# A two-layer attention kernel: the row shift moved to GpSimd, strided row maxima, and another order of the third slot

## The chip, the cores and the metric

One core of one Trainium2 chip runs the kernel; its seven other cores do nothing. The metric is the device time of one launch in microseconds. The times stand in a table below.

## What is computed

32 batches of 256 rows of 256 numbers go through two layers. Layer 0 is cross-attention (16 heads of 64, 77 keys per batch) and a gated feed-forward part, layer 1 is cross-attention with other weights and a matrix product with quantised operands. Ahead of each part the rows are normalised:

```python
def _layernorm(x, axis=-1, eps=1e-05):
    m = jnp.mean(x, axis=axis, keepdims=True)
    v = jnp.var(x, axis=axis, keepdims=True)
    return (x - m) / jnp.sqrt(v + eps)

x = x + _L0_xattn_ref(_layernorm(x, axis=-1), ctx_768, ...)   # softmax(q k^T / 8) v, then Wo and bo
x = x + _L0_ffn_ref(_layernorm(x, axis=-1), ...)              # (silu(x wg^T) * (x wu^T)) wd^T, hidden size 768
x = x + _L1_xattn_ref(_layernorm(x, axis=-1), ctx_768, ...)
x = x + _L1_ffn_ref(_layernorm(x, axis=-1), L1_ffn_rhs)       # rows scaled by max|x|/127, rounded, times rounded rhs
```

## The kernel before, in words

A first block loads and splits the weights and computes keys and values of all batches for both layers. The second block is the part that this case is about. Every number in single precision is held as a high half (float16) and a low half (the rest), so that most products are three matmuls: high by high, low by high, high by low.

The second block runs 66 **bodies**, h = 0 to 65. Bodies 0 to 31 attend in layer 0, bodies 32 to 63 in layer 1. A body has four **slots**, u = 0 to 3, and each slot takes four of the sixteen heads, a **unit**. Work is pipelined over slots and bodies. In slot u, TensorE computes

- the scores of unit u (`scores`, line 1211), into a buffer that has to be emptied by the exponentials of the unit before;
- the queries of the unit two slots on (`queries`, through `product`, line 328);
- the output projection of the unit four slots back (`project`);
- the product of probabilities and values of the unit three slots back (`weigh_values`, line 1245).

DVE takes the negated row maxima of the scores in two halves (`nmax`, line 1513), the reciprocals of the row sums (`rden`, 1518) and the low halves `oT_l` and `qT_l`. ACT computes the exponentials with their sums (`ex`, 1390), and high halves of everything (line 343). POOL (GpSimd) turns exponentials into probabilities: times the reciprocal into `pr` (1681), the cast into `p` (1694), the rest into the low half of `p` (1686). SP's queue turns the probabilities by a DMA transpose into `pT` (line 1099), once for each half of the rows.

Beside attention, a layer-0 body carries the feed-forward part of older batches: of batch h - 2 the gate products 0 to 3 and of batch h - 3 the gate products 4 and 5 and the two down products. One gate product is `gate_up(c)`, chunk c of 128 of the 768 hidden columns: matmuls of `wgT` and of `wuT` with `x2T`. After it come `tanh_gate` on ACT (`th`, 1370), `sigmoid_gate` and `hidden` on DVE (`sg`, 1480; `hf`, 1491), `high_hidden` on ACT (`hT_h`) and `low_hidden` on POOL or DVE (`hT_l`). `down(t)` multiplies by `wdT`, and `out_rows` adds it to `y` on DVE (1501).

The path of a batch through a body is this. At the end of slot 3 DVE adds projection and residual into `x1` (line 1661). It waits there for POOL's copy of the `x1` before into `y` (1723). Statistics follow (`spreads`, `moments`, lines 373 to 381), then on POOL the power -1/2 (`inverse`, line 396), on DVE the normalised rows `x2` (`normalise_rows`, 368), then `x216` in two halves (ACT 343, DVE 357), and a DMA transpose on SP into `x2T` (`turn_second_rows`, line 1107), which all gate products of that batch read. `x_pair` (lines 1177, 347) holds the first rows of a batch that is to enter, which ACT normalises with the scale `rs` and the shift `nmr`; `xT` (line 312) is their transpose.

`shift` makes `nmr`, minus mean times inverse deviation, on DVE (line 386), for the entering rows and for the rows `yn` that layer 0 hands on.

In layer 1, DVE computes `x2`, its row maxima `am` (1616), the scale `lsc` (1506) and its reciprocal `linv` (1509) in slot 1; ACT scales the rows into `q_a` (1424), DVE rounds them (`q_i`, 1553), TensorE turns and multiplies them.

The order of everything is written out by hand: each engine walks the slots, and inside a slot the `if u == ...` lines stand in the order in which its instructions run. No engine reorders. Banks of PSUM for queries, gate, down and turned products come from a plan made by `uses` and `released`; two banks serve the feed-forward products in turn.

## Time and profile before

| | us |
|---|---|
| median of 3 runs | 1621.58 |
| lowest and highest | 1621.55, 1623.29 |
| time of the profiled execution | 1628.16 |
| its span, first to last instruction | 1626.0 |
| TensorE matmul busy | 1522.9 (94%) |
| DVE busy | 1406.7 (87%) |
| ACT busy | 1315.0 (81%) |
| POOL busy | 1273.6 (78%) |
| mean granted TensorE clock | 0.993 |

A busy time is the time in which the engine has an instruction at work; an instruction may begin up to 0.1 us before the one ahead of it ends. The first 180 us or so are the first block. Bodies of layer 0 fill the time to about 1030, bodies of layer 1 the rest.

### The profile page before, as it was taken

The numbers are of one execution on the slowest core, as the hardware profiler recorded it, in microseconds if no ns is written. First come the engines' busy times: TensorE is split into PE (matmuls) and PEld (weight loads), VectorE is DVE, ScalarE is ACT, GpSimd is POOL, SyncE is SP. The second block draws the span as 40 slices with busy tenths as digits, with TensorE's granted clock in tenths as the row PEclk, the third lists the DMA queues.
The fourth block names the chain that finished last, engine by engine and source line by source line (L and its number), as shares of the span: only waits on it lengthen the run. The fifth ranks groups of instructions, "written<-read, shape, count | busy, mean of one in ns | idle before, by whom it ended". The sixth has DMA issues, their size and how long they took to land.

```text
span 1626.0 us, 74813 instructions
## 1 busy us (share of the span) xinstructions
PE 1522.9 (94%) x27282; PEld 1318.8 (81%) x27282; DVE 1406.7 (87%) x3585; ACT 1315.0 (81%) x5514; POOL 1273.6 (78%) x1893
## 2 busy tenths in 40 slices
PE   7999888999999999999999999999999999999995
PEld 4556578899998999899999889888788888788883
DVE  6777678899999999999999978889989989998986
ACT  6656588888888888888888878788888888888883
POOL 5100188899999999999999888788888888888884
PEclk9999999999999999999999999999999999999998
DMA  9997699887887787787788989898888888888995
GB/s 261 358 294 260 212 184 180 172 184 167 176 182 169 174 182 165 177 179 170 176 178 170 169 156 174 171 187 184 186 182 187 188 188 188 183 186 183 190 179 117
DMA packets 740021, 307.76 MB, mean 189 GB/s; under 512 B 629201, under 2 KB 725361, under 8 KB 737841
## 3 DMA queue, kind: packets, MB, share of 16 engines
q1 hardware_dynamic: 738049, 299.32, 83.0%
q0 software_dynamic: 1840, 6.82, 1.5%
q8 instruction: 67, 1.10, 0.3%
q14 instruction: 65, 0.53, 0.1%
HBM read 87.09 MB, written 65.54 MB: 94 GB/s over the span
## 4 chain that ended last, share of the span: by engine, by line
POOL 30%; DVE 19%; issue 14%; PE 12%; ACT 9%; DMA 3%; SPq 1%; DVEq 1%; POOLq 0%; ACTq 0%
POOL pr L1681 11%; ACT ex L1390 8%; PE psum L328 7%; POOL p L1694 6%; POOL p L1686 5%; POOL hT_l L1672 3%; PE psum L1211 3%; DVE qT_l L360 3%; DVE oT_l L357 3%; POOL rs L396 2%; DVE x L368 2%; DVE nmax L1513 2%; POOL x_res L1705 2%; DMA pT<-p 2%; DVE ya L1604 1%
## 5 line engine op out<-in xcount | busy, mean ns | idle before, releaser
L1390 ACT ACTIVATE ex<-psum,nmax 128x77 f32<-128x77 f32 x2048 | 634.7, 331 | 47.8 <-DVE nmax L1513 38.3
L1390 ACT ACTIVATION_READ_ACCUMULATOR ex<-psum,nmax 128x1 f32 x2048 | 433.6, 212 | 0.0
L1686 POOL TENSOR_TENSOR p<-pr,p 128x308 f16<-128x308 f32 x512 | 398.5, 779 | 38.3
L1681 POOL TENSOR_TENSOR pr<-ex,rden 128x308 f32<-128x308 f32 x512 | 390.4, 763 | 29.7 <-DVE rden L1518 29.5
L328 PE MATMUL psum<-xT,wq_h 128*64 128x256 f16 x4064 | 353.4, 276 | 0.0
L1694 POOL CAST p<-pr 128x308 f16<-128x308 f32 x509 | 247.4, 486 | 45.6 <-DMA pT<-p 13.6
L1513 DVE TENSOR_REDUCE nmax<-psum 128x4 f32<-128x308 f32 x512 | 236.8, 463 | 53.2 <-PE psum L1211 51.7
L328 PE MATMUL psum<-xT,wq_l 128*64 128x256 f16 x2032 | 281.0, 273 | 0.0
L328 PE MATMUL psum<-wo_h,oT_h 128*64 128x256 f16 x1792 | 249.9, 275 | 28.0 <-DVE oT_l L357 27.8
L328 PE MATMUL psum<-wo_l,oT_h 128*64 128x256 f16 x1792 | 248.4, 273 | 0.0
L328 PE MATMUL psum<-wo_h,oT_l 128*64 128x256 f16 x1792 | 248.4, 273 | 0.0
L328 PEld LDWEIGHTS psum<-xT,wq_h 128*64 128x64 f16 x4064 | 211.2, 110 | 12.2
L1245 PE MATMUL psum<-pT,vb 77*64 77x256 f16 x3072 | 212.4, 273 | 4.4 <-DMA pT<-p 4.3
L343 ACT ACTIVATE oT_h<-psum 128x512 f16<-128x512 f32 x256 | 153.6, 600 | 62.4 <-PE psum L1245 59.1
L1211 PEld LDWEIGHTS psum<-kb,qT_h 64*128 64x128 f16 x4096 | 114.7, 94 | 88.1 <-issue 88.1
L357 DVE TENSOR_TENSOR oT_l<-psum,oT_h 128x512 f16<-128x512 f32 x256 | 174.2, 681 | 2.6 <-ACT oT_h L343 2.6
L1245 PEld LDWEIGHTS psum<-pT,vb 77*64 77x64 f16 x3072 | 164.2, 109 | 14.6 <-issue 11.8
L1211 PE MATMUL psum<-kb,qT_h 64*128 64x77 f16 x4096 | 145.4, 197 | 31.4 <-ACT ex L1390 12.8
L360 DVE SCALAR_TENSOR_TENSOR qT_l<-psum,qT_h 128x512 f16<-128x512 f32 x256 | 173.9, 679 | 0.0
L343 ACT ACTIVATE qT_h<-psum 128x512 f16<-128x512 f32 x256 | 152.0, 594 | 3.0 <-PEq L406 3.0
L396 POOL TENSOR_TENSOR rs<-ve,half_neg 128x2 f32<-128x2 f32 x127 | 88.6, 697 | 81.0 <-DVE ve L381 78.0
L328 PEld LDWEIGHTS psum<-wo_h,oT_h 128*64 128x64 f16 x1792 | 102.1, 110 | 47.2 <-DVE oT_l L357 42.3
(164 smaller groups left out, 3477.6 us busy)
## 6 DMA issues: line engine op xcount, KB each, us to landing
keys<-ks SPq DMA_DIRECT2D x16, 1232.0 KB, 6.8
kb<-keys SPq DMA_DIRECT2D x256, 77.0 KB, 2.7
vb<-vals SPq DMA_DIRECT2D x128, 154.0 KB
vals<-vs SPq DMA_DIRECT2D x64, 256.0 KB, 4.1
x_pair<-in_x_dram SPq DMA_DIRECT2D x32, 256.0 KB, 3.0
pT<-p SPq DMA_TRANSPOSE x512, 3.2
x_res<-in_x_dram SPq DMA_DIRECT2D x32, 256.0 KB, 3.1
mid_x<-y SPq DMA_DIRECT2D x32, 256.0 KB, 2.4
```

The source lines that it names most:

```text
L328: last = pe.matmul(o[b * DH:(b + 1) * DH], w[:, b * DH:(b + 1) * DH], x, **flags)
L343: return act.activation(dst, src, ACT.Copy, scale=scale)
L357: return dve.tensor_tensor(dst, src, hi, ALU.subtract)
L360: return dve.scalar_tensor_tensor(out=qT_l[i][:, :, :], in0=src, scalar=Q_DOWN, in1=qT_h[i][:, :, :], op0=ALU.mult, op1=ALU.subtract)
L396: pool.tensor_tensor(rs[:, :], ve[:, :], half_neg[:, :], ALU.pow).then_inc(s_inv[k], 1)
L1211: last = pe.matmul(SC[:, b, at], w[rows, a, t * P:(t + 1) * P], kb[u // 2][rows, b, part, u % 2 * PPU + a, :], start=(q == 0), stop=(q == ...
L1245: last = pe.matmul(o[b * DH:(b + 1) * DH, a, :].rearrange("p (t q) -> p t q", q=P), vb[u // 2][:, part, c:c + DH], pT[u][0:NK, b, at:at + ...
L1390: last = act.activation(ex[i][:, t, b, :], SC[:, t, b * NK:(b + 1) * NK], ACT.Exp, bias=nmax[i][:, t, b:b + 1], accum_out=den[i][:, t, b:b ...
L1513: dve.tensor_reduce(nmax[i][:, t, :], SC[:, t, :].rearrange("p (h k) -> p h k", k=NK), AX_X, ALU.max, negate=True).then_inc(s_m, 1)
L1681: pool.tensor_tensor(pr[:, t, :, :], ex[i][:, t, :, :], r, ALU.mult).then_inc(s_p, 1)
L1686: pool.tensor_tensor(d[:, t, 1, :, 0:NK], pr[:, t, :, :], d[:, t, 0, :, 0:NK], ALU.subtract).then_inc(s_pl, 1)
L1694: pool.tensor_copy(p16[v % 2][:, t, 0, :, 0:NK], pr[:, t, :, :]).then_inc(s_ph, 1)
```

## The change

`shift` goes from DVE to POOL and takes two instructions there: minus the mean, and that times the inverse deviation, with a semaphore of its own (`s_neg`) between them. It stands directly behind `inverse` for the entering rows and for `yn`. POOL's `inverse` and `shift` of the entering rows come after the probabilities of slot 1 and not before them.

The row maxima `am` are written and read with a stride of two numbers.

In layer 0 the third slot (u = 2) is in another order. Gate product 0 leaves slot 1 and comes in slot 2, after queries and `down(0)`. The output projection stands before `down(1)` and gate product 1. On DVE the maxima, `oT_l` and the second maxima come first, then the statistics of the entering rows, the reciprocals, `qT_l`, and then `out_rows(0)` and the elementwise parts of gate product 0. On ACT both sets of exponentials come first. On DVE in slots 0 and 1, the low half of `x216` goes from the end of slot 0 to slot 1, and SP's `turn_second_rows` from slot 0 to the end of slot 1.

In layer 1, `normalise_rows` goes from slot 1 to slot 0, and `am`, `lsc`, `linv` stand before the low half of `xT`.

The core of the diff:

```diff
-        def shift(dve, k, mv, rs, count):
-
-            dve.wait_ge(s_inv[k], count)
-            dve.scalar_tensor_tensor(out=nmr[k][:, :], in0=mv[:, :, 0], scalar=-1.0, in1=rs[:, :],
-                                     op0=ALU.mult, op1=ALU.mult).then_inc(s_nmr[k], 1)
+        def shift(pool, k, mv, rs, count):
+
+            pool.tensor_scalar(nmr[k][:, :], mv[:, :, 0], -1.0, None, ALU.mult).then_inc(s_neg[k], 1)
+            pool.wait_ge(s_inv[k], count)
+            pool.wait_ge(s_neg[k], count)
+            pool.tensor_tensor(nmr[k][:, :], nmr[k][:, :], rs[:, :], ALU.mult).then_inc(s_nmr[k], 1)
...
-        am = sb("am", [P, QT], F32)
+        am = sb("am", [P, QT, 2], F32)
...
                         if turning:
                             turn_probabilities(n + u - 1, (u - 1) % UNITS, 0)
-                        if u == 0 and lay[-2] == 0:
-                            turn_second_rows(h - 2)
...
                         if turning:
                             turn_probabilities(n + u - 1, (u - 1) % UNITS, 1)
+                        if u == 1 and lay[-2] == 0:
+                            turn_second_rows(h - 2)
...
-                        if u == 1 and lay[-2] == 0:
-                            pe.wait_ge(s_x2d, 16 * (h - 1))
-                            if like == 2:
-                                pe.wait_ge(s_kvf, RING + LATE_BASE + LATE - 1)
-                            gate_up(0, bank("gu", 0))
...
+                        if u == 2 and lay[-2] == 0:
+                            pe.wait_ge(s_x2d, 16 * (h - 1))
+                            if like == 2:
+                                pe.wait_ge(s_kvf, RING + LATE_BASE + LATE - 1)
+                            gate_up(0, bank("gu", 0))
...
-                        if u == 0 and lay[-2] == 0:
-                            dve.wait_ge(s_x216h, h - 1)
-                            low(dve, x216[:, :, 1, :], x2[:, :, :], x216[:, :, 0, :]).then_inc(s_x216l, 1)
...
+                        if u == 1 and lay[-2] == 0:
+                            dve.wait_ge(s_x216h, h - 1)
+                            low(dve, x216[:, :, 1, :], x2[:, :, :], x216[:, :, 0, :]).then_inc(s_x216l, 1)
...
-                        if u == 1 and lay[-2] == 1 and like <= NB:
-                            normalise_rows(dve, 1, x2, x1, mv2, rs2, h - 1, s_x2)
...
+                        if u == 0 and lay[-2] == 1 and like <= NB:
+                            normalise_rows(dve, 1, x2, x1, mv2, rs2, h - 1, s_x2)
```

Three places, as the instructions stand in each engine's queue. The first is SP's queue in a layer-0 body, from the keys' load of slot 0 to the last probability transpose of slot 1 (`p_1` holds odd units, `p_0` even ones). Before:

```order
L302 DMA kb<-keys 64x616 x2
L1099 DMA_TRANSPOSE pT<-p_1 128x8x128
L1107 DMA_TRANSPOSE x2T<-x 128x8x128
L312 DMA_TRANSPOSE xT<-x 128x8x128
L1099 DMA_TRANSPOSE pT<-p_1 128x8x128
L1099 DMA_TRANSPOSE pT<-p_0 128x8x128
L1084 DMA vb<-vals 77x2x512
L1099 DMA_TRANSPOSE pT<-p_0 128x8x128
```

And now:

```order
L303 DMA kb<-keys 64x616 x2
L1100 DMA_TRANSPOSE pT<-p_1 128x8x128
L313 DMA_TRANSPOSE xT<-x 128x8x128
L1100 DMA_TRANSPOSE pT<-p_1 128x8x128
L1100 DMA_TRANSPOSE pT<-p_0 128x8x128
L1085 DMA vb<-vals 77x2x512
L1100 DMA_TRANSPOSE pT<-p_0 128x8x128
L1108 DMA_TRANSPOSE x2T<-x 128x8x128
```

The transpose into `x2T` has moved past `xT`, three probability transposes and the values' load.

The second is TensorE's queue in the layer-0 loop, around gate product 0. Before, it lies between the value product of slot 1 and the scores of slot 2:

```order
L328 MATMUL psum<-wo_l,oT_h 64x256 x2
L1245 MATMUL psum<-pT,vb 64x256 x12
L1347 REGISTER_ALU
L1293 REGISTER_ALU
L328 MATMUL psum<-x2T,wgT 64x256 x8
L328 MATMUL psum<-x2T,wuT 64x256 x8
L1198 REGISTER_ALU
L270 REGISTER_ALU
L1211 MATMUL psum<-kb,qT_h 128x77 x4
```

And now, between `down(0)` and the output projection of slot 2:

```order
L329 MATMUL psum<-wdT,hT_h 64x256 x2
L329 MATMUL psum<-wdT,hT_l 64x256 x2
L1320 REGISTER_ALU
L1294 REGISTER_ALU
L329 MATMUL psum<-x2T,wgT 64x256 x8
L329 MATMUL psum<-x2T,wuT 64x256 x8
L1220 REGISTER_ALU
L329 MATMUL psum<-wo_h,oT_h 64x256 x2
```

The gate product has moved behind the scores, the queries and the first down product.

The third is DVE's queue in the layer-1 loop, from `qT_l` of slot 0. Before:

```order
L360 SCALAR_TENSOR_TENSOR qT_l<-psum,qT_h 128x512
L1518 RECIPROCAL rden<-den 128x4 x2
L1512 ISA
L1513 TENSOR_REDUCE nmax<-psum 128x4
L1548 REGISTER_ALU
L357 TENSOR_TENSOR oT_l<-psum,oT_h 128x512
L1512 REGISTER_ALU
L1513 TENSOR_REDUCE nmax<-psum 128x4
L1599 REGISTER_ALU
L360 SCALAR_TENSOR_TENSOR qT_l<-psum,qT_h 128x512
L368 TENSOR_SCALAR x<-x,mv,rs 128x256 x2
```

And now:

```order
L361 SCALAR_TENSOR_TENSOR qT_l<-psum,qT_h 128x512
L369 TENSOR_SCALAR x<-x,mv,rs 128x256 x2
L1519 RECIPROCAL rden<-den 128x4 x2
L1513 ISA
L1514 TENSOR_REDUCE nmax<-psum 128x4
L1536 REGISTER_ALU
L358 TENSOR_TENSOR oT_l<-psum,oT_h 128x512
L1513 REGISTER_ALU
L1514 TENSOR_REDUCE nmax<-psum 128x4
L1586 REGISTER_ALU
L361 SCALAR_TENSOR_TENSOR qT_l<-psum,qT_h 128x512
L1607 TENSOR_REDUCE am<-x 128x2
```

The two rows of the normalisation (`x<-x,mv,rs`) have moved ahead of slot 1's maxima.

## Rows read from the trace of the kernel before

**Rows 1.** Busy time in a stretch of layer 0: PE, PEld, DVE, ACT, POOL, clock, DMA

```profile
400.00:500.00 100.00, 97.85 (x1956) 91.39 (x1952) 91.03 (x253) 87.19 (x368) 91.91 (x135) 1.00 0.80 175
```

**Rows 2.** Timeline of DVE, layer 0, two bodies' ends: start, duration, instruction

```profile
507.52 0.69 DVE L1661 SCALAR_TENSOR_TENSOR x<-psum,x_res 128x512 f32<-128x512 f32 x1 [0.24 <-POOL y L1723]
...
532.06 0.69 DVE L1661 SCALAR_TENSOR_TENSOR x<-psum,x_res 128x512 f32<-128x512 f32 x1 [0.23 <-POOL y L1723]
```

**Rows 3.** Timeline of POOL, the same body of layer 0, slots 0 and 1

```profile
509.88 0.69 POOL L396 TENSOR_TENSOR rs<-ve,half_neg 128x2 f32<-128x2 f32 x1 [0.48 <-DVE ve L381]
...
518.01 0.67 POOL L1672 TENSOR_TENSOR hT_l<-hf,hT_h 128x256 f16<-128x256 f32 x1 [0.34 <-ACT hT_h L343]
518.64 0.75 POOL L1686 TENSOR_TENSOR p<-pr,p 128x308 f16<-128x308 f32 x1
```

**Rows 4.** Timeline of TensorE, layer 1: projection and scores that waited

```profile
1309.50 0.30 PE L328 MATMUL psum<-wo_h,oT_h 128*64 128x256 f16 x2 [0.64 <-DVE oT_l L357]
...
1312.44 0.25 PE L1211 MATMUL psum<-kb,qT_h 64*128 64x77 f16 x4 [0.34 <-ACT ex L1390]
```

**Rows 5.** Timeline of DVE, layer 0, x216 and hidden chunk 5

```profile
513.33 1.10 DVE L357 TENSOR_TENSOR x<-x 128x512 f16<-128x512 f32 x1
...
517.06 0.42 DVE L1491 SCALAR_TENSOR_TENSOR hf<-psum,sg 128x256 f32<-128x256 f32 x1
```

**Rows 6.** Timeline of SP's queue, layer 0: issue of the transposes

```profile
514.45 1.23 SPq L1107 DMA_TRANSPOSE x2T<-x  x1
...
517.12 2.72 SPq L1099 DMA_TRANSPOSE pT<-p  x2
...
520.49 1.23 SPq L1099 DMA_TRANSPOSE pT<-p  x1
```

**Rows 7.** Tile x2T, from 340 to 880: DMA from issue to landing

```profile
DMA to landing us min/median/max: 3.2/3.2/3.6
```

**Rows 8.** Timeline of TensorE, layer 0, slot 2 (first row of each part)

```profile
518.75 0.24 PE L1211 MATMUL psum<-kb,qT_h 64*128 64x77 f16 x4
...
520.62 0.39 PE L328 MATMUL psum<-xT,wq_h 128*64 128x256 f16 x4
...
521.93 0.28 PE L328 MATMUL psum<-wdT,hT_h 128*64 128x256 f16 x2
...
523.24 0.60 PE L328 MATMUL psum<-x2T,wgT 128*64 128x256 f16 x8
...
524.11 0.28 PE L328 MATMUL psum<-wo_h,oT_h 128*64 128x256 f16 x2
...
525.42 0.82 PE L1245 MATMUL psum<-pT,vb 77*64 77x256 f16 x12
526.18 0.24 PE L1211 MATMUL psum<-kb,qT_h 64*128 64x77 f16 x4
```

**Rows 9.** Timeline of ACT, layer 0: tanh and high parts of hidden chunks

```profile
501.23 0.42 ACT L343 ACTIVATE hT_h<-hf 128x256 f16<-128x256 f32 x1 [0.22 <-DVE hf L1491]
...
505.63 0.36 ACT L1370 ACTIVATE th<-psum 128x256 f32<-128x256 f32 x1
...
524.32 0.38 ACT L1370 ACTIVATE th<-psum 128x256 f32<-128x256 f32 x1 [0.51 <-PE psum L328]
...
525.75 0.42 ACT L343 ACTIVATE hT_h<-hf 128x256 f16<-128x256 f32 x1 [0.22 <-DVE hf L1491]
```

**Rows 10.** Busy time in four microseconds near 940, columns of rows 1

```profile
940.00:944.00 4.00, 4.00 (x60) 3.48 (x58) 1.89 (x6) 2.64 (x11) 2.90 (x4) 0.57 0.97 196
```

**Rows 11.** Timeline of TensorE, the wait ahead of that

```profile
938.88 0.63 PE L328 MATMUL psum<-x2T,wgT 128*64 128x256 f16 x8 [1.86 <-DMA x2T<-x]
```

**Rows 12.** Line L577, a small addition on POOL: duration min/median/max in ns

```profile
L577 POOL TENSOR_TENSOR ve<-mv,eps x1: 191/191/191, 165.5 to 165.5; 128x2 f32<-128x2 f32 x1
```

**Rows 13.** Line L368, the normalised rows, whole trace: duration min/median/max in ns

```profile
L368 DVE TENSOR_SCALAR x<-x,mv,rs x126: 401/634/996, 237.3 to 1603.0; 128x256 f32<-128x256 f32 x126
```

**Rows 14.** Timeline of DVE, layer 1: first maxima of slot 1

```profile
1302.81 0.48 DVE L1513 TENSOR_REDUCE nmax<-psum 128x4 f32<-128x308 f32 x1 [0.72 <-PE psum L1211]
```

More of the change, by code:

```diff
@@ L280, in xattn_ffn_kernel @@
         s_inv = [sem(f"s_inv{i}") for i in range(3)]
+        s_neg = [sem(f"s_neg{i}") for i in range(3)]
         s_nmr = [sem(f"s_nmr{i}") for i in range(3)]
@@ L580, in _ @@
                 inverse(pool, 0, ve1, rs1, 1)
+                shift(pool, 0, mv1, rs1, 1)
             @block.scalar
@@ L1010, in uses @@
                         out.append(("turned_x", 0))
-                    if lay[-2] == 0:
-                        out.append(("gu", 0))
                 if u == 2:
@@ L1015, in uses @@
                         out.append(("down", 0))
+                    if lay[-2] == 0:
+                        out.append(("gu", 0))
                     if lay[-3] == 0:
@@ L1301, in body @@
                             scores(n + u, u, 32 * (h + 1))
-                        if u == 2 and lay[-3] == 0:
-                            pe.wait_ge(s_hlp, len(LOW_POOL) * (h - 2))
-                            pe.wait_ge(s_hld, len(LOW_DVE) * (h - 2))
-                            down(0, bank("down", 0))
                         if u == 3 and lay[-2] == 0:
@@ L1317, in body @@
                                 quantised(t, bank("quant", t))
+                        if u == 2 and lay[-3] == 0:
+                            pe.wait_ge(s_hlp, len(LOW_POOL) * (h - 2))
+                            pe.wait_ge(s_hld, len(LOW_DVE) * (h - 2))
+                            down(0, bank("down", 0))
+                        if u == 2 and lay[-2] == 0:
[3 more added lines that the diff above has]
+                            gate_up(0, bank("gu", 0))
                         if u == 0 and lay[-3] == 0:
@@ L1337, in body @@
                             project(n + u - 4, u, four)
+                        if u == 2 and lay[-3] == 0:
+                            down(1, bank("down", 1))
+                        if u == 2 and lay[-2] == 0:
+                            if like == 2:
+                                pe.wait_ge(s_kvf, RING + LATE_BASE + LATE)
+                            gate_up(1, bank("gu", 1))
                         if u == 2 and lay[-2] == 1:
@@ L1455, in body @@
                             exponentials(n + u, u % 2, 1)
+                        if u == 2 and lay[-2] == 0:
+                            tanh_gate(0, h - 2)
+                        if u == 2 and lay[2] == 0:
+                            act.wait_ge(s_nmr[0], h + 2)
+                            act.wait_ge(s_x16l, h + 1)
+                            normalise(act, xn, x_in, rs1, 0, s_xn)
                         if u == 1 and lay[-3] == 0:
@@ L1600, in body @@
                             low_q(dve, (u + 1) % 2, RG[(u + 1) % 2]).then_inc(s_ql, 1)
+                        if u == 2 and lay[-3] == 0:
+                            out_rows(0)
+                        if u == 2 and lay[-2] == 0:
+                            sigmoid_gate(0, h - 2)
+                        if u == 2 and lay[-2] == 0:
+                            hidden(0, h - 2)
+                        if u == 1 and lay[-2] == 0:
+                            dve.wait_ge(s_x216h, h - 1)
+                            low(dve, x216[:, :, 1, :], x2[:, :, :], x216[:, :, 0, :]).then_inc(s_x216l, 1)
+                        if u == 1 and lay[-3] == 0:
+                            sigmoid_gate(5, h - 3)
+                        if u == 1 and lay[-3] == 0:
+                            hidden(5, h - 3)
+                        if u == 1 and lay[-3] == 0:
+                            low_hidden(4, h - 3)
+                        if u == 0 and lay[-2] == 1 and like <= NB:
+                            normalise_rows(dve, 1, x2, x1, mv2, rs2, h - 1, s_x2)
+                        if u == 1 and lay[-2] == 1 and like <= NB:
+                            dve.wait_ge(s_x2, QT * (h - 1))
+                            dve.tensor_reduce(am[:, :, 0], x2[:, :, :], AX_X, ALU.max,
+                                              apply_absolute_value=True).then_inc(s_am, 1)
+                            quantising_scale(h - 2 - B)
                         if u == 3 and lay[-2] == 1:
@@ L1723, in body @@
                             pool.tensor_copy(y[:, :, :], x1[:, :, :]).then_inc(s_yx, 1)
-                        if u == 1 and lay[2] == 0:
-                            inverse(pool, 0, ve1, rs1, h + 2)
                         if (like, u) == (NB - 1, 3):
@@ L1730, in body @@
                             probabilities(h, u, 0)
+                        if u == 1 and lay[2] == 0:
+                            inverse(pool, 0, ve1, rs1, h + 2)
+                            shift(pool, 0, mv1, rs1, h + 2)
                         if u == 2 and lay[-3] == 0:
                             inverse(pool, 2, ve3, rs3, h - 2)
+                            shift(pool, 2, mv3, rs3, h - 2)
                         if u == 2 and lay[-2] == 0:
```

55 lines of the change are left out of this document (11 added, 44 removed).

## The prediction

> **What bounds the kernel now.** I read the stretches first, then one body of each layer on each engine, then who waited for whom. In layer 0 the matmuls cover 97.9% of a stretch at full granted clock [rows 1], so little can be gained there: the additions into `x1` of two neighbouring bodies stand at 507.52 and 532.06, a body of 24.6 us with the clock at 1.00, and in both DVE waits 0.2 us for POOL's copy into `y` [rows 2]. TensorE, DVE and POOL are all nearly full, so what matters is no engine's sum but the loop that a body closes over several engines: `x1`, its row statistics, the inverse deviation on POOL (509.88, it waited for DVE's `ve` [rows 3]), POOL's probabilities in program order, the pieces of the feed-forward part, the next `x1`. Layer 1 has slack on every engine and loses time in small waits, such as 0.64 us before the output projection and 0.34 us before the scores [rows 4].
>
> **The turn of the second rows (layer 0).** This is the main term. `x2T`, the turned second rows, is what every gate product reads. Before, SP issues that transpose in the first slot, at 514.45, as soon as DVE has `x216`. Now it stands behind the second probability transpose of the second slot. That one waits for POOL's last piece of unit 0, and SP takes its queue strictly in order. When is that piece ready? POOL's inverse starts at 509.88, 2.36 us after `x1`. From there POOL works in order until the subtraction of 518.64, 0.75 us long, ends at 519.39: 9.51 us [rows 3]. POOL's `hT_l` ahead of it (518.01) needs the hidden chunk 5 of DVE, 517.06. DVE's 1.10 us subtraction `x216` moves from 513.33 to a place in front of that chunk. DVE then idles first, for the scores of unit 1; I estimate +0.3 us [rows 5]. Then the `pT` transpose occupies SP 1.25 us (520.49), `x2T` follows it, and lands 3.2 us after its start [rows 6, 7]. From `x1` to the first possible gate product: 2.36 + 9.51 + 0.3 + 1.3 + 3.2 + 0.1 for the hand-overs = **16.8 us**, that is 524.3 on the clock of these rows.
>
> When would TensorE like to have it? The first gate product (0.87 us, as 523.24 to 524.11) no longer stands ahead of the scores at 518.75. They move up by it and by some 0.45 us of waits in unit 1 (DVE's `x216` had stood in front of that unit's maxima), to about 517.4. Scores and one down product take 1.87 us, queries 1.31, so the gate product's turn comes at 520.6 [rows 8]. It waits 3.7 us in an in-order queue, with output projection, second down and gate product, and value product all behind it.
>
> The loop from there: gate 0.87, projection 1.31, down 1.31 until the second gate product starts (3.5); 1.08 to its tanh (523.24 to 524.32), 1.43 to the high part of the second hidden chunk (525.75), 4.40 from such a copy to the last tanh of the fourth slot (501.23 to 505.63), 1.65 to `x1` (507.52 without the 0.24 us for POOL) [rows 2, 8, 9]. 16.8 + 3.5 + 1.08 + 1.43 + 4.40 + 1.65 = 28.9 us, the upper end. The lower end counts the lateness once: second slot ends at 524.3 + 0.87 + 1.31 + 1.31 + 0.87 + 0.76 = 529.4 instead of 526.18, +3.3, less the 0.24 us: 27.7. The difference is that the second gate product now stands right before the value product, so its elementwise chain starts later against the fourth slot. I take 28.3, since small waits inside the upper chain can close: **+3.7 us a body**. 31 bodies hold this product, and one or two next to the change of layers already have slack: 30 x 3.7 = **+111 us** (ends 93 and 129).
>
> **TensorE's clock.** A stop of 3.7 us (part of it taken earlier, before the queries) in every body is new. Around 938.88 the trace has one wait of 1.86 us for this very transpose, and the granted clock of the next four microseconds is 0.57, so nearly all at 1.2 GHz [rows 10, 11]. At 0.57 in 4 us, 4 x (1 - 0.57) = 1.7 us of work are lost, and what follows the wait is the critical chain. I take it for six bodies in ten: 30 x 0.6 x 1.7 = **+30 us** (ends 0 and 51). The Trainium skill, TensorE: Matmul & The Clock Gate, section HAM oscillation, tells of a kernel whose every tile waits for a DMA, and whose every next tile starts at half clock; by that rule all 30 bodies would pay, +51 in place of +30, and the forecast would be 1771. The same page, Part 1, puts the ramp under 1% of a typical kernel, at most some 16 us here; by that 1736. No row here has a regularly repeated stop.
>
> **Mean times inverse deviation on POOL.** Two per layer-0 body: DVE loses two small instructions, POOL gains four, with a wait of its own between them. The nearest rows are POOL's 128x2 addition at 0.19 us and the 128x2 power at 0.69 [rows 3, 12]: 0.8 to 2.8 us a body. In the old loop this would be serial, since DVE waits for POOL's `y` at `x1`. In the longer loop POOL gets idle time ahead of the third inverse, which now waits for later statistics. I book 0, and up to 0.5 us a body at the dearer end (+15 on the high side).
>
> **Layer 1.** The normalisation of the second rows moves from behind the maxima of unit 1 to the end of unit 0, and scale and reciprocal come ahead of `xT`. The pair of rows costs 2 x 0.63 us at the median, 2 x 0.40 or 2 x 1.00 at the ends [rows 13]. It lands in the 0.72 us that DVE idles before the maxima at 1302.81 [rows 14], and starts after POOL's inverse, about 1302.2. So these maxima start at 1303.6, 0.8 us late; unit 1's exponentials and the next scores follow by as much. Against that the scale is ready over a microsecond earlier, so ACT no longer waits for it in unit 2. The projection at 1309.50 waited for DVE [rows 4] and starts as before; the exponentials of unit 2 end before TensorE asks, so the 0.34 us before 1312.44 and about 0.1 beside them go: -0.42 us a body, 30 bodies, **-13 us**. At 0.40 a row everything moves up by half a microsecond more, about -1.0 a body (-29); at 1.00 it turns to +0.14 (+4). The strided maxima save part of a small instruction that is off this path: 0.
>
> **Sum.** +111 + 30 - 13 = +128 against the profiled execution's own 1628.2, which is 6.6 us over the median; against the median, 1621.6 + 128 = **1750 us**.
>
> **The rivals.**
> - The turn is late, but the clock holds: 1621.6 + 111 - 13 = 1720. For it: other stretches with waits stay at full clock. Chance 0.28.
> - POOL is what counts: `x2T` comes in time after all, because POOL runs ahead, and only the four small instructions lengthen POOL's loop, by 0.8 us at least: 1621.6 + 24 - 13 = 1633, and 1690 at the dearer price. Against it: POOL waits for `ve` at 509.88 in each body, so it can't run ahead of `x1`. Chance 0.09.
> - Faster. The mechanism is the third slot itself: with maxima first and gate product behind, 0.45 us of waits a body go. It decides if SP issues `x2T` by 517.3, 3.3 us ahead of 520.6; SP would then need POOL's piece by 516.0, 3.4 us before 519.39 [rows 3]. The price: 1621.6 - 30 x 0.45 - 13 = 1595. Chance 0.07.
> - It does nothing measurable: turn and shorter waits cancel. 1621, chance 0.03.
>
> **How the numbers follow.** The forecast (late turn and half clock in many bodies) has 0.53, and with its bounds spans about 1725 to 1790. 1690 to 1785 takes in the clock that holds and the lower end of the loop (1621.6 + 93 - 29 = 1686), and leaves the cases below and the dearest sum out. A difference of 0.2%, some 3 us, is what a measurement of this kernel can tell from none. Faster by more than that 0.07, within it 0.03, slower 0.90.
>
> **What would show it.** In the profile after: layer-0 `x1` additions 28 us apart or more; TensorE idle before a gate product with the DMA into `x2T` as releaser, about 3 us in each body; SP's `x2T` directly behind a `pT`, some 13.5 us after `x1`; granted clock under 1.00 in layer 0's stretches; layer-1 bodies near 18.5 us; ACT's wait for the scale gone. If the bodies of layer 0 stay under 25 us, the loop as I drew it is wrong; if TensorE waits for `x2T` but the clock reads 1.00, only the clock term falls.

## The result, and the profile after

The changed kernel takes **1786.73 us** (median of 5 runs, 1783.84 to 1795.86) against 1621.55 us of the kernel before in the same job. The ratio is 1.102, with a 95% interval of 1.1001 to 1.104: 165 us slower. 1750 was forecast, with a range of 1690 to 1785. The sign, the place and the main mechanism are as forecast; the size lies 1.7 us above the range, and the profiled execution, 1795.86 us, 11 us above it.

The stretches come first, one of each layer (columns as in [rows 1]: length, PE, PEld, DVE, ACT, POOL busy, granted clock, DMA share, GB/s).

```profile
400.00:500.00 100.00, 82.39 (x1518) 75.97 (x1516) 67.57 (x190) 66.46 (x285) 77.01 (x124) 0.94 0.66 144
1400.00:1500.00 100.00, 95.76 (x1843) 83.55 (x1840) 92.89 (x232) 85.00 (x410) 87.83 (x137) 1.00 0.87 192
```

Layer 0 lost 15 us of TensorE's 98 in a hundred and has a granted clock of 0.94 where [rows 1] had 1.00. Everything is less busy, POOL too (77 where it was 92): no engine became the bound, a wait did. Layer 1 gained. The chain that ended last (first by engine, then its largest lines) says the same, with a DMA among the lines:

```profile
POOL 28%; issue 18%; PE 16%; DVE 9%; SPq 9%; DMA 7%; ACT 2%; POOLq 0%; DVEq 0%; ACTq 0%
PE psum L329 14%; POOL pr L1680 11%; POOL p L1693 7%; SPq L1100 6%; DMA x2T<-x 6%; POOL p L1685 4%; POOL rs L391 2%; SPq L313 2%; POOL hT_l L1671 2%; DVE x L369 1%; PE psum L1212 1%; DMA pT<-p 1%; DVE sg L1481 1%; POOL y L1722 1%; DVE x L1660 1%
```

The waits of the whole span (who waited for whom, us in total, times, longest):

```profile
ACT th L1371 <- PE psum L329: 261.9, 65, 6.3
POOL rs L391 <- DVE ve L382: 232.1, 96, 15.4
...
PE psum L329 <- DMA x2T<-x: 106.5, 32, 4.1
```

32 waits of TensorE for `x2T`, 3.3 us each: one in every body of layer 0. ACT's and POOL's sums were 56.2 and 78.0 us before; the body below shows both waiting in the wake of the same stop.

One body of layer 0 in the timelines, of DVE (its two `x1` additions; answers to [rows 2]), POOL ([rows 3]), SP ([rows 6]), TensorE ([rows 8]) and ACT ([rows 9]), with start, duration and, in brackets, idle time before and what ended it:

```profile
568.89 0.69 DVE L1660 SCALAR_TENSOR_TENSOR x<-psum,x_res 128x512 f32<-128x512 f32 x1 [0.24 <-POOL y L1722]
...
599.29 0.69 DVE L1660 SCALAR_TENSOR_TENSOR x<-psum,x_res 128x512 f32<-128x512 f32 x1 [0.24 <-POOL y L1722]
```

```profile
571.25 0.72 POOL L391 TENSOR_TENSOR rs<-ve,half_neg 128x2 f32<-128x2 f32 x1 [0.48 <-DVE ve L382]
...
579.89 0.67 POOL L1671 TENSOR_TENSOR hT_l<-hf,hT_h 128x256 f16<-128x256 f32 x1 [1.11 <-ACT hT_h L344]
580.51 0.76 POOL L1685 TENSOR_TENSOR p<-pr,p 128x308 f16<-128x308 f32 x1
...
583.90 0.22 POOL L395 TENSOR_SCALAR nmr<-mv 128x2 f32<-128x2 f32 x1
584.27 0.20 POOL L398 TENSOR_TENSOR nmr<-nmr,rs 128x2 f32<-128x2 f32 x1
584.42 1.26 POOL L1704 TENSOR_TENSOR x_res<-x_res,bo_b 128x512 f32<-128x512 f32 x1
...
594.13 1.12 POOL L391 TENSOR_TENSOR rs<-ve,half_neg 128x2 f32<-128x2 f32 x1 [4.46 <-DVE ve L382]
```

```profile
581.37 1.24 SPq L1100 DMA_TRANSPOSE pT<-p  x1
582.71 1.29 SPq L1108 DMA_TRANSPOSE x2T<-x  x1
```

```profile
580.00 0.41 PE L329 MATMUL psum<-xT,wq_h 128*64 128x256 f16 x4 [0.82 <-DMA xT<-x]
...
586.04 0.63 PE L329 MATMUL psum<-x2T,wgT 128*64 128x256 f16 x8 [3.24 <-DMA x2T<-x]
586.50 0.98 PE L329 MATMUL psum<-x2T,wuT 128*64 128x256 f16 x8
```

```profile
587.60 0.38 ACT L1371 ACTIVATE th<-psum 128x256 f32<-128x256 f32 x1 [4.37 <-PE psum L329]
...
592.30 0.38 ACT L1371 ACTIVATE th<-psum 128x256 f32<-128x256 f32 x1 [3.35 <-PE psum L329]
```

The body is 30.40 us long, where it was 24.54. POOL's last piece of unit 0 ends at 581.27, SP turns it at 581.37, and only then `x2T`, at 582.71, 13.8 us after `x1` (forecast 13.5). The first gate product stands at 586.04, 17.15 us after `x1` (forecast 16.8), after a stop of 3.24 us. And it runs slow: eight products of `wuT` take 0.98 us where eight of this shape took 0.60 in [rows 8]. The clock of four-microsecond stretches of this body shows it:

```profile
580.00:584.00 4.00, 2.81 (x48) 2.54 (x48) 3.34 (x11) 3.23 (x18) 3.86 (x7) 1.00 0.99 198
584.00:588.00 4.00, 1.96 (x24) 1.83 (x26) 0.00 (x0) 0.40 (x2) 3.70 (x7) 0.82 0.87 174
588.00:592.00 4.00, 4.00 (x60) 3.80 (x58) 1.38 (x4) 0.96 (x2) 1.52 (x3) 0.75 0.35 66
592.00:596.00 4.00, 4.00 (x90) 3.74 (x86) 3.76 (x12) 3.43 (x12) 1.72 (x4) 1.00 0.68 171
```

4 x (1 - 0.82) + 4 x (1 - 0.75) = 1.7 us of work are lost, the same 1.7 as taken from [rows 10]. In stretches of one microsecond the clock reads 0.96 from 586 to 587, 0.50 in each of the next three, and 1.00 from 590 on: it falls to 1.2 GHz behind the stop, when TensorE is already at work again.

In how many bodies does the clock fall? Of the 33 distances between neighbouring `x1` additions in layer 0, 28 are between 29.3 and 31.2 us and five are under 29. The granted clock from one `x1` to the next tells it directly: it is 0.89 to 0.95 in 30 of the 33 bodies, and 1.00 in three of 28.6 to 28.9 us. This is the profiled execution, 9 us above the median, with a mean granted clock of 0.960 where the other four have 0.965 to 0.969, so in the median execution some bodies fewer will have fallen.

The length of the stop doesn't tell a body that falls from one that does not. The first of these two gate products of the changed kernel belongs to a body with the clock at 1.00, the second to one with 0.94:

```profile
526.87 0.63 PE L329 MATMUL psum<-x2T,wgT 128*64 128x256 f16 x8 [3.14 <-DMA x2T<-x]
...
920.22 0.63 PE L329 MATMUL psum<-x2T,wgT 128*64 128x256 f16 x8 [3.15 <-DMA x2T<-x]
```

Layer 1 has bodies of 18.37 us against 18.87 to 18.95 before.

### The profile page after: what moved, and what is told of

Its sections match the earlier page's. It is cut to its first block, busy times and chain, and to the rows that moved or that the text cites. A ratio compares the mean times of both kernels' runs of the same rounds, so it can differ in the third digit from the quotient of the medians.

```text
span 1793.9 us, 74939 instructions
## 1 busy us (share of the span) xinstructions
PE 1576.5 (88%) x27282; PEld 1360.7 (76%) x27282; DVE 1379.9 (77%) x3522; ACT 1295.0 (72%) x5514; POOL 1287.2 (72%) x2019
## 3 DMA queue, kind: packets, MB, share of 16 engines
q8 instruction: 68, 1.11, 0.3%
## 4 chain that ended last, share of the span: by engine, by line
POOL 28%; issue 18%; PE 16%; DVE 9%; SPq 9%; DMA 7%; ACT 2%; POOLq 0%; DVEq 0%; ACTq 0%
PE psum L329 14%; POOL pr L1680 11%; POOL p L1693 7%; SPq L1100 6%; DMA x2T<-x 6%; POOL p L1685 4%; POOL rs L391 2%; SPq L313 2%; POOL hT_l L1671 2%; DVE x L369 1%; PE psum L1212 1%; DMA pT<-p 1%; DVE sg L1481 1%; POOL y L1722 1%; DVE x L1660 1%
## 5 line engine op out<-in xcount | busy, mean ns | idle before, releaser
L1391 ACT ACTIVATION_READ_ACCUMULATOR ex<-psum,nmax 128x1 f32 x2048 | 454.4, 222 | 0.0
L1680 POOL TENSOR_TENSOR pr<-ex,rden 128x308 f32<-128x308 f32 x512 | 382.4, 747 | 22.7 <-DVE rden L1519 22.6
L329 PE MATMUL psum<-wo_h,oT_h 128*64 128x256 f16 x1792 | 265.8, 291 | 8.1 <-DVE oT_l L358 6.1
L1693 POOL CAST p<-pr 128x308 f16<-128x308 f32 x509 | 237.0, 466 | 45.3 <-DMA pT<-p 13.2
L391 POOL TENSOR_TENSOR rs<-ve,half_neg 128x2 f32<-128x2 f32 x127 | 100.2, 789 | 232.5 <-DVE ve L382 232.1
L1371 ACT ACTIVATE th<-psum 128x256 f32<-128x256 f32 x192 | 75.8, 395 | 262.0 <-PE psum L329 261.9
L329 PE MATMUL psum<-wo_h,oT_l 128*64 128x256 f16 x1792 | 263.8, 289 | 0.0
L329 PE MATMUL psum<-wo_l,oT_h 128*64 128x256 f16 x1792 | 262.9, 288 | 0.0
L329 PE MATMUL psum<-x2T,wgT 128*64 128x256 f16 x1536 | 123.8, 285 | 106.5 <-DMA x2T<-x 106.5
L1481 DVE SCALAR_TENSOR_TENSOR sg<-th,psum 128x256 f32<-128x256 f32 x192 | 79.4, 413 | 156.6 <-ACT th L1371 154.1
```

Of the source, the lines that this page charges most:

```text
L329: last = pe.matmul(o[b * DH:(b + 1) * DH], w[:, b * DH:(b + 1) * DH], x, **flags)
L391: pool.tensor_tensor(rs[:, :], ve[:, :], half_neg[:, :], ALU.pow).then_inc(s_inv[k], 1)
L1391: last = act.activation(ex[i][:, t, b, :], SC[:, t, b * NK:(b + 1) * NK], ACT.Exp, bias=nmax[i][:, t, b:b + 1], accum_out=den[i][:, t, b:b ...
L1680: pool.tensor_tensor(pr[:, t, :, :], ex[i][:, t, :, :], r, ALU.mult).then_inc(s_p, 1)
L1693: pool.tensor_copy(p16[v % 2][:, t, 0, :, 0:NK], pr[:, t, :, :]).then_inc(s_ph, 1)
```

## The experiments

No kernel below leaves any of the computation out; `fill_wait` and `fill_dve` do additional products whose output nothing reads. Three dots in a diff stand for lines of it that are not shown. "Body" is the median distance between two `x1` additions of layer 0 in the profiled execution: 24.6 us before, 30.4 after.

**1. fill_wait: the clock alone.** The late turn stays; 20 products of weights by weights stand ahead of the wait for `x2T`, in the same PSUM bank, which the gate product then starts anew.

```diff
-pe.wait_ge(s_x2d, 16 * (h - 1))
...
+o = bank("gu", 0)
+for _ in range(20):
+    product(pe, o[:, 0, :], wgT[:, 0, 0:P], wuT[:, 0, 0:2 * P], True, start=True, stop=True)
+pe.wait_ge(s_x2d, 16 * (h - 1))
-gate_up(0, bank("gu", 0))
+gate_up(0, o)
```

> The changed kernel with 20 products of weights by weights (about 2.2 us of TensorE time, overwritten by the real product) put ahead of the wait for the turned second rows in layer 0's third slot. They fill the stop, nothing else is earlier. If the half clock after the stop costs what the trace of the changed kernel shows (bodies of 30.4 us, a few of 28.7), every body comes to about 28.7 us, the granted clock in layer 0 to 1.00, and the time to 1787 - 27 x 1.7 = about 1741. If the clock's dip is hidden under other waits, the time stays at 1787. The wait for the DMA falls from 3.2 us to about 1 either way.

Measured: 1741.39 us (1739.29 to 1743.66), ratio 1.0732 (1.0704 to 1.076), body 28.7 us. The stretch of layer 0, and one body's gate product with the next `x1` additions:

```profile
400.00:500.00 100.00, 92.10 (x1844) 86.23 (x1838) 78.08 (x213) 76.52 (x332) 81.85 (x132) 1.00 0.66 147
```

```profile
506.86 0.63 PE L329 MATMUL psum<-x2T,wgT 128*64 128x256 f16 x8 [0.85 <-DMA x2T<-x]
...
518.45 0.69 DVE L1663 SCALAR_TENSOR_TENSOR x<-psum,x_res 128x512 f32<-128x512 f32 x1 [0.24 <-POOL y L1725]
547.20 0.69 DVE L1663 SCALAR_TENSOR_TENSOR x<-psum,x_res 128x512 f32<-128x512 f32 x1 [0.24 <-POOL y L1725]
```

More work on TensorE, and 45 us less time: the clock reads 1.00, and from gate product to next `x1` it takes 11.6 us (518.45 - 506.86) where after takes 13.25 (599.29 - 586.04). The clock's share of the loss is 45 us, by the medians of the runs. What remains of the stop is 0.85 us here, 0.85 to 1.6 in the middle bodies and up to 2.6 near the two ends of the layer. Over whole bodies the clock is 1.00 in 31 of the 33; it is 0.94 and 0.95 in two near the ends. So the waits alone now set the length, all but some 3 us of it (2 x 1.7).

**2. early_turn: the late turn undone.** `turn_second_rows` on SP and the low half of `x216` on DVE go back to slot 0; all else stays changed.

```diff
+if u == 0 and lay[-2] == 0:
+    turn_second_rows(h - 2)
...
-if u == 1 and lay[-2] == 0:
-    turn_second_rows(h - 2)
...
```

> The changed kernel with the turn of the second rows (SP) and the low half of x216 (DVE) back in slot 0; the third slot's new order, the shift on POOL and layer 1 as changed. My theory: TensorE's stop for the turned rows and the low clock go, and all but some of the 165 us come back. What is left is told apart by two forecasts: if POOL's four small instructions (about 1.0 us a body in the changed kernel's trace) lie in the loop, bodies are about 25.5 us and the time 1621.6 + 30 - 15 = about 1636; if the third slot's order saves what I took (0.45 us) and POOL has room, about 1595. A rival that blames the third slot's order itself (second gate product late against slot 3) has bodies over 27 us and over 1690.

Measured: 1661.93 us (1657.03 to 1665.29), ratio 1.0245 (1.0214 to 1.0275), body 26.2. 125 of the 165 us were the late turn, and 80 of these (1741.4 - 1661.9) without the clock. But it stays 26 us above the theory's 1636, with bodies of 26.2 us, 1.6 above the kernel before, where the theory had 25.5: some 0.7 us a body are in something else. Its waits from 350 to 850 us name a candidate:

```profile
PE psum L329 <- DMA xT<-x: 16.6, 20, 1.0
...
DVE x L1660 <- POOL y L1722: 4.5, 19, 0.2
```

TensorE waits 0.8 us in each body for the entering rows' transpose, since the queries now come ahead of `down(0)`; and `x1` waits for POOL's `y`, as it does in [rows 2] and in the changed kernel's body above.

**3. turn_before_pT: one place on SP.** The changed kernel, with `turn_second_rows` ahead of the second probability transpose of slot 1 instead of behind it.

```diff
+if u == 1 and lay[-2] == 0:
+    turn_second_rows(h - 2)
 if turning:
     turn_probabilities(n + u - 1, (u - 1) % UNITS, 1)
-if u == 1 and lay[-2] == 0:
-    turn_second_rows(h - 2)
```

> The changed kernel with only two neighbours on SP exchanged: the transpose of the second rows before the second probability transpose of slot 1, not behind it. It no longer waits for POOL's last piece of unit 0, nor for that transpose's 1.25 us of issue. In the changed kernel's trace it would go at about 581.3 and not at 582.7, so TensorE's stop shrinks from 3.2 to about 1.8 us. If lateness passes one to one into the body: -1.4 us each, 1787 - 42 = 1745; if the shorter stop also keeps the clock up in most bodies: a further -1.7 us each, about 1700. If the queue's order were not the cause: 1787.

Measured: 1722.46 us (1718.6 to 1722.88), ratio 1.0611 (1.0585 to 1.0638), between the two values. Most bodies are 27.3 to 28.1 us, and about every fourth is 29.3 to 30.6. TensorE still waits (from 350 to 850 us):

```profile
PE psum L329 <- DMA x2T<-x: 40.8, 18, 2.7
```

That is 2.3 us a time, where 1.8 was expected. One step in SP's order is worth 64 us. By the two profiled executions up to 37 of these are the clock's: it is 0.94 in 8 of the 33 bodies, where the changed kernel has 30 at 0.95 or less, and 22 x 1.7 = 37. Here too the stop's length doesn't pick the bodies: one of 29.28 us (clock 0.94) has a stop of 2.06 us, one of 28.06 (clock 1.00) a stop of 2.56.

**4. shift_on_dve: POOL's four small instructions undone, under the late turn.** `shift` as in the kernel before, on DVE.

```diff
-shift(pool, 0, mv1, rs1, h + 2)
-shift(pool, 2, mv3, rs3, h - 2)
...
+shift(dve, 0, mv1, rs1, h + 2)
+shift(dve, 2, mv3, rs3, h - 2)
...
```

> The changed kernel with mean times inverse deviation back on DVE, two instructions a body instead of POOL's four. My theory: POOL idles 4.5 us a body ahead of the third inverse in the changed kernel, so this changes nothing: 1787, within 6 us. The rival that POOL's longer loop is the cause: -1 us a body, about 1757 or less.

Measured: 1774.59 us (1770.71 to 1779.47), ratio 1.0924 (1.0892 to 1.0955): 12 us less than the changed kernel, twice the 6 us that the theory allowed. The bodies come in threes in a good part of the trace, two of 30.1 to 30.6 and one of 28.4, and the clock of a body is at 0.95 or less in 23 of the 33, not 30, though the stops are as long as in the changed kernel (107.4 us in 32 waits, there 106.5). So part of the 12 us is the clock's. Run 9 takes the two apart.

**5, 6. layer1_alone and layer1_strided.** The kernel before with the change's order in layer 1 only (the maxima and the scale move ahead of `xT`'s low part too), and the same with the strided maxima.

```diff
-if u == 1 and lay[-2] == 1 and like <= NB:
+if u == 0 and lay[-2] == 1 and like <= NB:
     normalise_rows(dve, 1, x2, x1, mv2, rs2, h - 1, s_x2)
...
```

> The kernel before, with the change's order in layer 1 alone: the second rows are normalised at the end of unit 0, and maxima, scale and reciprocal stand ahead of xT's low part; the maxima stay dense, layer 0 is untouched. The trace after the change has layer-1 bodies of 18.37 us where before had 18.9, so 0.54 us less in each of 30. If that part adds up on its own: 1621.6 - 16 = 1605 us, within 3 us. Rival: layer 1's bodies are shorter only because the slower layer 0 hands it work in another phase; then 1618 to 1622.

> The same kernel with the maxima strided as well, every second element of a buffer twice as wide. In the trace after the change the scale (128x2) still takes 0.64 us at the median, where it took 0.69 before; its fastest ones take 0.17. Theory: the stride does nothing, the scale stays near 0.64 to 0.69 us and the time is that of layer1_alone within 2 us. Rival: the stride lets the scale go at its 0.17 us once layer 0 does not run late; it stands behind the maxima and ahead of xT's low part, so up to 0.5 us in each of 30 bodies, 15 us less than layer1_alone.

Measured: 1610.62 us (1606.46 to 1614.62), ratio **0.9933** (0.991 to 0.9955), and 1611.3 us (1607.18 to 1617.4), ratio 0.9936 (0.9913 to 0.996). Layer 1's part is real and stands on its own: bodies of 18.37, 10 us in all and not the 16 expected. The 0.5 us is gained in 23 of 30 bodies; those at the layer's two ends were short before. The stride does nothing: the scale has its median at 0.636 us in both kernels. The scale in the strided kernel, and the POOL instruction beside it:

```profile
1313.76 0.70 POOL L1681 TENSOR_TENSOR pr<-ex,rden 128x308 f32<-128x308 f32 x1
```

```profile
1313.84 0.63 DVE L1506 TENSOR_SCALAR lsc<-am 128x2 f32<-128x2 f32 x1
```

The scale, 128x2, takes 0.63 us and ends at 1314.47; POOL's product, begun 0.08 us ahead of it, ends at 1314.46. In the kernel before it was 0.70 us from 1307.45, to 1308.15, beside a POOL subtraction that ended at 1308.12. At the program's end (1618.18 in the kernel before), where POOL does nothing, it takes 0.17.

**7. shift_on_pool.** The kernel before with `shift` on POOL and nothing else (the reverse of the diff of run 4).

> The kernel before, with mean times inverse deviation moved to POOL alone, both places in layer 0. In the trace after the change the pair takes 1.0 us from issue to issue for two of them each body. Theory: POOL's loop through y, x1 and the statistics is closed in the kernel before (DVE waited 0.2 us for y in both bodies read), so most of it is paid: 30 x 0.8 to 1.0 = 24 to 30 us, 1646 to 1652. Rival: only the first of the two lies in the loop, or neither: 1622 to 1636. This also sets how much of the 1.5 us a body that early_turn leaves above the kernel before is POOL's.

Measured: 1641.69 us (1640.51 to 1645.42), ratio 1.0118 (1.0094 to 1.0142), body 25.4: +0.8 us a body, 21 us. The pair on POOL (busy, mean ns of one):

```profile
L395 POOL TENSOR_SCALAR nmr<-mv 128x2 f32<-128x2 f32 x63 | 14.5, 229 | 0.0
L398 POOL TENSOR_TENSOR nmr<-nmr,rs 128x2 f32<-128x2 f32 x63 | 12.6, 200 | 9.4 <-POOL nmr L395 0.2
```

In the changed kernel's body above a pair starts at 583.90 and the instruction behind it at 584.42: 0.5 us a pair, two pairs a body. In a loop that closes through POOL's order nearly all of it is paid.

**8. early_dve.** early_turn with `shift` on DVE too; of layer 0's change the third slot is left, and with it two smaller moves that no run takes apart from it: POOL's inverse for the entering rows behind a piece of probabilities, and DVE's `hT_l` of chunk 4 behind hidden chunk 5.

> early_turn with mean times inverse deviation back on DVE: what remains of the change in layer 0 is the third slot (maxima first, queries ahead of the first down product, first gate product behind it) and the order on DVE. early_turn stood at 1661.9 with bodies of 26.1 us, 1.5 above the kernel before. Theory: 1.0 of that 1.5 is POOL's loop, so 30 us go: about 1632 us. Rival: what is left is the third slot's own, TensorE at the queries waiting for the first rows' transpose (1.0 us in about every body): then it gains 10 us at most, 1652 or more.

Measured: 1642.22 us (1640.74 to 1652.99), ratio 1.0146 (1.0112 to 1.0179), body 25.6: between theory and rival. The shift on POOL is 0.6 us of early_turn's body (20 us); 1.0 us a body, above layer1_alone as well as above the kernel before, is the third slot's, with those two moves.

**9. fill_dve.** fill_wait with `shift` on DVE.

> fill_wait (20 dummy products ahead of the wait for the turned second rows, so that the clock holds) with mean times inverse deviation back on DVE. fill_wait stood at 1741.4 with bodies of 28.7 us, where the prediction's sum has 28.3. Theory: the 0.4 us between is POOL's four small instructions, as the 12 us of shift_on_dve: bodies of 28.3 us, 1741 - 12 = 1729. Rival: they are hidden once TensorE waits, and shift_on_dve's 12 us came by the clock (one body in three kept it): then 1741, bodies still 28.7.

Measured: 1734.47 us (1732.76 to 1739.96), ratio 1.0699 (1.0667 to 1.0731), body 28.4: 7 us less than fill_wait, between theory and rival. The price of POOL's four instructions is 21 us in the kernel before, 20 with the early turn, 7 when TensorE waits for a transpose: once the loop has another bound, most of it hides. Of the 12 us of run 4 this leaves 5 for the clock. The split is rough: seven bodies fewer with a lowered clock would make 12 us at 1.7 each, and the two profiled executions are 16 us apart.

**10. early_dve_down.** early_dve with `down(0)` ahead of the queries again.

```diff
+if u == 2 and lay[-3] == 0:
+    pe.wait_ge(s_hlp, len(LOW_POOL) * (h - 2))
+    pe.wait_ge(s_hld, len(LOW_DVE) * (h - 2))
+    down(0, bank("down", 0))
 if ("q", u) in plan:
```

(and gone from behind them)

> early_dve with one thing more: the first down product stands ahead of the queries in the third slot again, as in the kernel before. early_dve has layer-0 bodies of 25.6 us against 24.55 before, and TensorE waits there 0.9 us for the transpose of the first rows (xT) ahead of the queries in each body read. Theory: this wait is the third slot's price; the down product (1.3 us, needing nothing new) fills it, bodies come to 24.6 to 24.8 and the time to 1642 - 30 x 0.9 = 1615 us, within 6, below the kernel before by the layer-1 part. Rival: the price is the order on DVE and ACT (the third slot's maxima and tanh), and the wait only moves: 1632 us or more.

Measured: 1638.28 us (1636.45 to 1639.85), ratio 1.0096 (1.007 to 1.0121), body 25.3. This is the rival's range; the theory's gain of 27 us became 4. The wait for `xT` is gone, and a wait for the hidden chunk's low part stands in its place, while ACT idles in the same slot:

```profile
503.98 0.30 PE L329 MATMUL psum<-wdT,hT_h 128*64 128x256 f16 x2 [0.53 <-POOL hT_l L1675]
```

```profile
507.78 0.39 ACT L1371 ACTIVATE th<-psum 128x256 f32<-128x256 f32 x1 [1.24 <-PE psum L329]
508.99 1.09 ACT L348 ACTIVATE x_pair<-x_pair,nmr,rs 128x256 f32<-128x256 f32 x2 [0.82 <-DVE nmr L396]
511.20 0.38 ACT L1371 ACTIVATE th<-psum 128x256 f32<-128x256 f32 x1 [1.11 <-PE psum L329]
```

ACT does all exponentials first and then idles three times, 3.2 us: twice for gate products that come late in the slot, and in the middle for DVE's `shift` of the entering rows. Before, the first product was ready from slot 1, and ACT had its tanh ahead of the exponentials. The middle one is new as well: from 350 to 850 us ACT idles 18.0 us in 20 waits for that `shift` here, and 0.6 us in 2 waits in the kernel before. `shift` takes 1.22 us there, beside a POOL instruction (the lines are in the last section). How much of the third slot's price hangs on it was not tested.

**11. gate_back.** early_dve_down with gate product 0 back at the end of slot 1 on TensorE; ACT and DVE keep the new order.

> early_dve_down with the first gate product back at the end of unit 1 on TensorE, where the kernel before has it; tanh, gate and hidden chunk on ACT and DVE stay where the change put them. early_dve_down has layer-0 bodies of 25.32 us, 0.78 above the kernel before, and in the third slot ACT idles 1.2, 0.8 and 1.1 us for TensorE and the statistics, where it idled 1.0 and 0.5 before. Theory: two gate products in one slot leave ACT and DVE without work first and with too much at its end, so the place of that product is the price: bodies of 24.6 to 24.8 us, 1638.3 - 30 x 0.65 = 1619, within 5. Rival: the order on ACT and DVE (maxima and exponentials ahead of the tanh) is the price: bodies stay at 25.2 or more, 1634 or more.

Measured: 1676.44 us (1674.63 to 1678.83), ratio 1.033 (1.0299 to 1.0361), body 26.7. A clear miss of the theory: it is 38 us worse than early_dve_down, more than the rival had too. TensorE, in slot 2 of that kernel:

```profile
522.13 0.30 PE L329 MATMUL psum<-wdT,hT_h 128*64 128x256 f16 x2 [1.57 <-DVE hf L1492]
```

TensorE now waits for DVE's hidden chunk `hf`. Since ACT and DVE take that gate product only behind the slot's exponentials and maxima, its results are read late, and what needs them or their room on TensorE waits (which of the two isn't told apart here). So the product's place and the order on ACT and DVE can't be undone singly. The 0.75 us a body that early_dve_down has above the kernel before belong to both together, and to what moved with them (run 8, and ACT's wait of run 10); undoing all of it is layer1_alone, with 24.5.

**12. layer1_early_y.** layer1_alone, with POOL's copy into `y` ahead of the last subtraction of its piece in slot 3.

```diff
 pool.tensor_copy(p16[v % 2][:, t, 0, :, 0:NK], pr[:, t, :, :]).then_inc(s_ph, 1)
+if early:
+    start_sum()
 low_of(b, v, t)
...
```

> layer1_alone with one thing more: in the fourth slot of layer 0 POOL's copy into y stands ahead of the last subtraction of that slot's first piece, not behind it. In the kernel before, DVE waits 0.23 us for that copy at the addition into x1 in nearly every body, and POOL then waits 0.48 us for the statistics. Theory: x1 moves up by 0.2 us a body, all of it kept, since POOL has the 0.48 us to lose: layer-0 bodies of 24.3, 1610.6 - 30 x 0.2 = 1604 to 1605. Rival: the loop closes elsewhere within a tenth (the probabilities that now turn 0.6 us later): 1610 to 1612, or up to 6 us more if the later turn is waited for.

Measured: 1606.04 us (1603.69 to 1609.53), ratio **0.9897** (0.9872 to 0.9922), in a job where the kernel before took 1622.54. The wait of `x1` for `y` is gone:

```profile
524.28 0.66 DVE L1661 SCALAR_TENSOR_TENSOR x<-psum,x_res 128x512 f32<-128x512 f32 x1
548.71 0.66 DVE L1661 SCALAR_TENSOR_TENSOR x<-psum,x_res 128x512 f32<-128x512 f32 x1
```

The body is 24.4, so 0.1 us shorter and not the full 0.2. It is the fastest kernel of the study, 1% ahead of the kernel before; its distance to layer1_alone comes from two jobs, and their intervals overlap a little (0.991 to 0.9955 against 0.9872 to 0.9922).

## Why the prediction was right, and where it was not

The medians of the runs form a chain from before to after: layer 1 alone 1610.6 (-11 against 1621.6), the third slot +32 (early_dve 1642.2), `shift` on POOL +20 (early_turn 1661.9), the late turn +79 (fill_wait 1741.4), the clock +45 (1786.7). The steps come from several jobs, in which the kernel before varied by 3 us, so each is good to a few us, and they hold in this order: under the late turn `shift` is worth 7 and not 20.

The forecast fell 37 us short. Two terms of its sum were too small, the loop by 20 us (131, not 111) and the clock by 15 (45, not 30), and layer 1 gave 10 or 11 where 13 was booked. Either of the first two misses alone would have stayed inside the range.

- **The turn of the second rows, +111: the path is right, the size 20 us short.** The sum stood for all that lengthens the loop with the clock held, and fill_wait measures that: +131 from layer1_alone (1741.4 - 1610.6). Its single steps held well: SP issues `x2T` 13.8 us after `x1` (13.5), the gate product stands at 17.0 to 17.15 (16.8), and from there to the next `x1` it takes 11.6 (11.5 taken, between 10.9 and 12.1). The +0.3 us for DVE's late hidden chunk was 0.77 (POOL's `hT_l` waits 1.11 us, 0.34 in [rows 3]). TensorE came to its turn at 582.80 (586.04 - 3.24), 13.9 us after `x1` and not 13.1, since it had waited 0.82 us for `xT`; so the stop was 3.24 us and not 3.7. And the 0.24 us by which `x1` waits for POOL's `y`, which the sum let go, stayed (568.89 and 599.29). A body of fill_wait is 28.7 us, where 28.3 was taken between 27.7 and 28.9, and 4.2 longer than one of layer1_alone (24.5), not 3.7: 30 times that difference is 14 of the 20 us. POOL's `shift`, booked at 0, is 0.3 us of each body: fill_dve, without it, has 28.4. The other 6 us lie in the bodies at the two ends and ahead of the first `x1`, where the traces of different kernels differ by as much (the first `x1` stands at 227.3 us in layer1_alone and at 231.6 in fill_wait).
- **What the +111 was put down to.** The forecast gave all of it to the late turn. With the rest of the change in place, undoing the turn takes 80 us off fill_wait and leaves 51 (early_turn against layer1_alone), which the third slot and `shift` cost when `x2T` is early. So the length of the loop was nearly right, and its cause in part wrong; that the booked price of the turn alone came so near to the whole is partly luck.
- **The third slot: the wrong sign, hidden by the late turn.** The prediction took its order as a gain of 0.45 us a body, and made it a rival. early_dve shows a loss of 1.0 us a body once `x2T` is early. The working had counted waits of unit 1 only, and not that queries would now ask for `xT` 1.3 us earlier (a wait of 0.8 us, whose removal in run 10 gave back 0.3). The rest goes with ACT's idle time in that slot, which the traces show and no run prices singly. The rival "faster, 1595" was therefore false even on its own condition: with the early turn the time is 1662, and 1642 without POOL's shift.
- **`shift` on POOL, booked at 0: 7 us under the late turn, 20 to 21 us else.** The prediction had both cases, and the upper bound of 15 us covers the first. That they would cost in the old loop, which POOL closes, was right.
- **TensorE's clock, +30: a share that rested on no row.** "Six bodies in ten" is the step that failed here; the 1.7 us a body was from a row, and right. The profiled execution has the lowered clock in 30 of 33 bodies, and 45 / 1.7 = 27 bodies by the medians. The Trainium skill, TensorE: Matmul & The Clock Gate, section HAM oscillation, by which every body would pay, comes near to the trace, with 30 of 33, and 1771 by that rule was nearer than the forecast. What the prediction drew from that page's ramp under 1% of a typical kernel, at most 16 us, does not hold here: 45 us are 2.5%. But all or nothing is no rule either: with a stop of about 2.3 us eight bodies in 33 fall (turn_before_pT), with mostly 0.85 to 1.6 us two (fill_wait), and with stops as long as in the changed kernel 23 (shift_on_dve). The share grows with the stop, and stops of 3.14 and 3.15 us differ in outcome; what picks the bodies stays open.
- **Layer 1, -13: right, a little large.** -10 in layer1_alone, and -11 by the sum of the 30 distances of layer 1 in the two traces (562.0 us before, 551.0 after). The strided maxima are 0, as booked.
- **The range.** Its upper edge of 1785 left out "the dearest sum" (1621.6 + 129 + 51 - 13 = 1789), and this is nearly what came: a loop of 131 and a clock of 45. The two are not independent: the runs with the longer stops have the clock down in more bodies.

## What to carry to other kernels

Before a transfer is issued later, ask behind which entries of an in-order queue it will stand and what the last of these waits for. One place ahead of a single probability transpose was worth 64 us here, and all of the late turn 125 of the 165. If a stop of TensorE recurs at the same place in each body, don't book the clock by a share that no row gives: take the case in which every body pays into the range (here 30 of 33 did, and in neighbouring kernels 23, 8 and 2), and test it by filling the wait with products that nobody reads. This run separates the wait from the clock at once. A change in many parts can hide a good one: layer 1's order, taken alone, makes the kernel 0.7% faster.

## What the runs showed of the hardware

- Filling a 3.2 us stop with 20 idle products saves 45 us of 1787, though TensorE does more. A body with a stop of 0.85 us in its place keeps the granted clock at 1.00; one of 3.24 us is followed by 0.82 and 0.75 in two stretches of four microseconds, with matmuls 1.6 times as long (0.98 us for eight that take 0.60). The length alone doesn't decide: a body with a stop of 2.06 us fell to 0.94, bodies with stops of 2.56 and 3.14 us kept 1.00.
- A small DVE instruction can be as long as its neighbour on POOL. The scale of 128x2 takes 0.17 us alone and 0.63 to 0.70 where it ends with POOL's instruction, within 0.03 us. It holds for the shift on DVE too, in early_dve_down:

```profile
507.59 1.27 POOL L1708 TENSOR_TENSOR x_res<-x_res,bo_b 128x512 f32<-128x512 f32 x1
507.66 1.22 DVE L396 SCALAR_TENSOR_TENSOR nmr<-mv,rs 128x2 f32<-128x2 f32 x1 [0.48 <-POOL rs L391]
```

  1.22 us for 128x2 numbers, ending at 508.88 with POOL's addition (508.86); the shortest of its kind in the kernel before took 0.15. The Trainium skill, SBUF — State Buffer, section SBUF: two separate sides, has VectorE and GpSimd share a port pair that one of them holds for a whole instruction, if the DVE instruction is in a two-port mode, or has two inputs in SBUF and the GpSimd one reads SBUF. The trace agrees for both instructions, the scale with one input and the shift with two; that the scale runs in such a mode is not visible in it. A stride of two elements did not free the scale (layer1_strided, 0.63).
- A pair of dependent 128x2 instructions on POOL takes 0.5 us from its start to that of the next instruction (583.90 to 584.42), and two pairs a body, 1.0 us, cost 0.8 in a loop that POOL closes (shift_on_pool).
